# An FFN behind a grouped convolution: differences of x blocks and the low half of the odd blocks formed by GpSimd

## The reference

```python
def cond(x, c, weight, c_weight, bias):          # x (32, 64, 1024), 4 groups, 9 taps, padding 4
    out = lax.conv_general_dilated(x, weight, (1,), [(4, 4)], feature_group_count=4, ...)
    return out + einsum('nd,od->no', c, c_weight)[:, :, None] + bias[None, :, None]

def ffn(h, A_w, B_w, Wq_w, keys):                # last axis 1024; 64 experts of rank 8, top 16
    q = einsum('bsd,rd->bsr', h, Wq_w)
    scores = einsum('bsr,er->bse', q, keys)
    top_vals, top_idx = lax.top_k(scores, 16)
    gate = scatter of softmax(top_vals) to the 64 experts, 0 elsewhere
    z = einsum('bsd,nd->bsn', h, A_w)            # 64 experts x 8
    return 2.0 * einsum('bsn,on->bso', z * gate (per expert), B_w)

x = x + ffn(cond(x, ...), ...)
```

## Time and profile before

| | |
|---|---|
| median of 3 runs | 234.09 us (233.68 to 234.31) |
| span of the profiled execution, first to last instruction | 232.1 us |
| TensorE busy | 227.8 us, 98% |
| VectorE busy | 194.5 us, 84% |
| ScalarE busy | 99.5 us, 43% |
| GpSimd busy | 1.5 us, 1% |

### The profile page before, as it was taken

One profiled execution on the slowest core, in us unless ns is written; L12 is line 12 of the kernel. 1 busy time (PEld: TensorE's weight loads), 2 busy tenths in 40 slices (PEclk: granted clock), 3 DMA queues, 4 the chain that ended last, 5 costly groups with the idle time before them and its releaser, 6 DMA issues.

```text
span 232.1 us, 4019 instructions
## 1 busy us (share of the span) xinstructions
PE 227.8 (98%) x1381; PEld 203.3 (88%) x1381; DVE 194.5 (84%) x471; ACT 99.5 (43%) x246; POOL 1.5 (1%) x10
## 2 busy tenths in 40 slices
PE   7999999999999999999999999999999999999995
PEld 7898998898989889898998989889898989898884
DVE  2799899999999899998999899898998979847232
ACT  4997768246262352525334262532536242101000
POOL 2000000000000000000000000000000000000000
PEclk9999999999999999999999999999999999999999
DMA  6999064742744628173462825538281343554532
GB/s 199 372 406 395 25 194 127 274 133 93 211 151 104 218 82 270 60 211 144 95 235 74 252 82 148 187 88 263 67 272 69 60 169 90 186 145 130 180 135 92
DMA packets 23781, 38.79 MB, mean 167 GB/s; under 512 B 2768, under 2 KB 11856, under 8 KB 23760
## 3 DMA queue, kind: packets, MB, share of 16 engines
q1 hardware_dynamic: 23616, 38.45, 51.5%
q10 hardware_dynamic: 144, 0.08, 0.2%
HBM read 25.94 MB, written 12.58 MB: 166 GB/s over the span
## 4 chain that ended last, share of the span: by engine, by line
PE 90%; ACT 6%; DMA 2%; issue 1%; SPq 0%; DVE 0%; ACTq 0%
PE p_z L646 35%; PE p_out L684 13%; PE p_out L685 13%; PE p_out L692 13%; PE p_conv L600 10%; ACT h_c L395 3%; PE p_out L646 3%; PE p_conv L543 3%; DMA x_blk<-in_x_blocks 2%; ACT x_hi L359 1%; ACT a_hi L359 1%; PE p_z L668 1%; ACT h_hi L359 0%; PE p_z L692 0%; PE p_z L684 0%
## 5 line engine op out<-in xcount | busy, mean ns | idle before, releaser
L684 PE MATMUL p_out<-b_hi,zt_hi 128*128 128x512 f32 (+1 forms) x128 | 50.1, 392 | 0.0
L685 PE MATMUL p_out<-b_hi,zt_lo 128*128 128x512 f32 (+1 forms) x128 | 50.1, 392 | 0.0
L692 PE MATMUL p_out<-b_lo,zt_hi 128*128 128x512 f32 (+1 forms) x128 | 34.4, 391 | 0.0
L646 PE MATMUL p_z<-a_hi,h_lo 128*128 128x264 f32 x240 | 34.2, 285 | 0.0
L646 PE MATMUL p_z<-a_hi,h_hi 128*128 128x264 f32 x240 | 34.1, 285 | 0.0
L646 PE MATMUL p_z<-a_lo,h_hi 128*128 128x264 f32 x240 | 33.9, 284 | 0.0
L646 PEld LDWEIGHTS p_z<-a_hi,h_hi 128*128 128x128 f32 x240 | 32.0, 188 | 1.6 <-issue 0.4
L646 PEld LDWEIGHTS p_z<-a_hi,h_lo 128*128 128x128 f32 x240 | 31.3, 188 | 0.0
L646 PEld LDWEIGHTS p_z<-a_lo,h_hi 128*128 128x128 f32 x240 | 31.0, 188 | 0.0
L685 PEld LDWEIGHTS p_out<-b_hi,zt_lo 128*128 128x128 f32 x128 | 24.0, 188 | 5.6
L684 PEld LDWEIGHTS p_out<-b_hi,zt_hi 128*128 128x128 f32 x128 | 24.0, 188 | 5.6
(11 more groups left out here) (105 smaller groups left out, 258.1 us busy)
## 6 DMA issues: line engine op xcount, KB each, us to landing
x_nat<-in_x_rows SPq DMA_DIRECT2D x16, 512.0 KB, 5.0
out_dram<-x_nat SPq DMA_DIRECT2D x31, 256.0 KB, 3.3
x_blk<-in_x_blocks SPq DMA_DIRECT2D x14, 516.0 KB, 4.0
z_dram<-a_raw SPq DMA_DIRECT2D x64, 64.0 KB, 1.8
a_raw<-z_dram SPq DMA_DIRECT2D x16, 256.0 KB, 3.7
a_raw<-in_a_wq SPq DMA_DIRECT2D x8, 264.0 KB, 6.1
x_nat<-in_b_w SPq DMA_DIRECT2D x4, 512.0 KB, 8.6
x_blk<-in_x_blocks SPq DMA_DIRECT2D x2, 258.0 KB, 3.6
```

Of the source, the lines that this page charges most:

```text
L646: mm = nc.tensor.matmul(z_bank(t, b)[:, 0:HB], h[:, t % 2, r, :], a[:, r, b * HB:(b + 1) * HB], start=k == 0 and r == 0, stop=k == 2 and r ...
L684: nc.tensor.matmul(dst, zt_hi[:, t % 2, c, :], b_hi[:, c, cols], start=c == 0, stop=False)
L685: nc.tensor.matmul(dst, zt_lo[:, t % 2, c, :], b_hi[:, c, cols], start=False, stop=False)
L692: mm = nc.tensor.matmul(dst, zt_hi[:, t % 2, c, :], b_lo[:, c, start:stop], start=False, stop=c == JC - 1)
```

## The change

`differ` moves from VectorE to GpSimd, for all eleven tiles from the sixth on. GpSimd also forms the low half of the odd blocks of these tiles (512 columns), under a semaphore of its own, `s_xlo_odd`; VectorE's instruction there covers only the two differences (1024 columns). `conv_sum` waits for the new semaphore, `conv_pair` for the old one. A load into a buffer whose last tile was such a tile also waits for it. GpSimd takes the tiles in order: two differences as soon as the blocks have come, then the low half once ScalarE's high half is there.

```diff
@@ SP
                     sp.wait_ge(*x_lo_done(t - XB))
+                if t >= XB + TW:
+                    sp.wait_ge(s_xlo_odd, t - XB - TW + 1)
@@ GpSimd
+            def differ(t, ab):
+                if ab == 0:
+                    pool.wait_ge(*x_come(t))
+                blocks = x_blk[:, t % XB]
+                nc.gpsimd.tensor_tensor(blocks[:, XS + ab * XO:XS + (ab + 1) * XO], blocks[:, ab * NN:ab * NN + XO],
+                                        blocks[:, XE:XS], ALU.subtract).then_inc(s_xd, 1)
+
+            def split_odd(t):
+                pool.wait_ge(s_xhi, x_split_count(t))
+                nc.gpsimd.tensor_tensor(x_lo[:, t % 2, 0:XO], x_blk[:, t % XB, XE:XS], x_hi[:, t % 2, 0:XO].bitcast(F32),
+                                        ALU.subtract).then_inc(s_xlo_odd, 1)
+
+            for t in range(TW, NT):
+                differ(t, 0)
+                differ(t, 1)
+                split_odd(t)
@@ TensorE, conv_products
-                    if x is x_lo:
+                    if x is x_lo and part == 0:
+                        pe.wait_ge(s_xlo_odd, t - TW + 1)
+                    if x is x_lo and part > 0:
                         pe.wait_ge(*x_lo_done(t))
@@ VectorE, split_x
-                low(x_part(x_lo[:, t % 2], t, half), x_raw(t, half), x_part(x_hi[:, t % 2], t, half), s_xlo)
+                if t < TW:
+                    low(x_part(x_lo[:, t % 2], t, half), x_raw(t, half), x_part(x_hi[:, t % 2], t, half), s_xlo)
+                else:
+                    low(x_lo[:, t % 2, XO:3 * XO], x_blk[:, t % XB, XS:XS + 2 * XO], x_hi[:, t % 2, XO:3 * XO], s_xlo)
@@ VectorE, its order
-            differ(5, 0)
-            differ(5, 1)
...
-                if i + 3 < NT:
-                    differ(i + 3, 0)
                 copy_scores(i)
                 top_first(i)
-                if i + 3 < NT:
-                    differ(i + 3, 1)
                 take_first(i)
```

More of the change, by code:

```diff
@@ L149, in adaln_ffn @@
         s_xlo = sem("s_xlo")
+        s_xlo_odd = sem("s_xlo_odd")
         s_xd = sem("s_xd")
@@ L778, in split_ws @@
                 low(ws_lo[:, g % 2], ws_raw[:, g], ws_hi[:, g % 2], s_wslo)
[L780 to L785, removed]
             def add_shared(t, ab):
```

## The result

| | before | after |
|---|---|---|
| median | 234.03 us (4 runs, 233.68 to 234.31) | 243.8 us (4 runs, 243.1 to 244.16) |
| span of the profiled execution | 232.1 us | 242.4 us |

What follows compares the result with a forecast made beforehand. The prediction took TensorE's queue to bound the kernel; 232.1 us of span plus 2.5 and 1.4 for meetings of GpSimd and VectorE gave 236.0, with 2.0 around the span 238.0 us, range 233.6 to 244.5.

Steps and rivals of the forecast that it cites:

- What bounds the kernel, and what VectorE's relief is worth: Whole kernel: it ends when TensorE's queue ends, so 20 us taken from VectorE gain 0.
- The smallest reserve: Between VectorE's end of `q_t` and TensorE's load of it for the scores: 0.57 us, taken for all steps concerned.
- GpSimd's instruction: Each two-input GpSimd instruction of 512 columns: 1.2 us, within bounds of 0.68 and 1.60.
- The shift of the block load: In each loop step, `neg_max` to `turn_z` and the block load behind it come 0.47 us earlier.
- The sign named for the shift: In the changed profile, `neg_max` starts 0.26 us behind the maxima.
- How many meetings, and which: Nine loop loads, tiles 7 to 15: five arrive just ahead of `h_lo`, four inside it.
- What a meeting costs: At `h_lo` and `q_t`: one whole GpSimd instruction where GpSimd comes first, less the reserve; 2.5 plus 1.4 us.
- the five steps: Loop steps whose blocks arrive just ahead of `h_lo`: 0.5 us lost in each, 2.5 us together.
- the four others: Loop steps whose blocks arrive inside `h_lo`: 0.7 us each or 0, charged by half, 1.4 us.
- The second rival: Both GpSimd differences go first, the second between `h_lo` and `q_t`; all four open steps pay: 245.8 us, chance 0.17.
- The part ahead of the loop: Sixth tile: GpSimd's low half of 1.2 us hidden by 2 us before the shared convolution, no loss.
- a slower GpSimd: Rival: GpSimd instructions take 1.6 us, 0.4 more in seven steps on average, 240.8 us, chance 0.10.

Runs made afterwards that it cites:

- e_from8: Changed kernel, but the sixth and seventh tile stay wholly with VectorE and GpSimd starts later tiles' differences only behind `q_t`: 234.25 us, ratio 1.0004.
- e_halves: Changed kernel with each GpSimd difference cut into two instructions of 256 columns: 234.78 us, ratio 1.0028.
- e_both: Changed kernel with GpSimd's differences placed: behind `q_t` from the eighth tile, at VectorE's old places for the sixth and seventh: 235.31 us, ratio 1.0047.

## Why the prediction was wrong

*What bounds the kernel, and what VectorE's relief is worth.* Right. e_from8 takes 10.8 us of busy time from VectorE, and the ratio is 1.0004.

*The smallest reserve.* Right in place, and in size for most steps: all nine waits of the loop are for `q_t`; a hold of 0.49 us is free in eight steps (e_halves), one of 1.04 costs 0.4. The forecast took one step's 0.57 us for all. In the kernel before it is 0.56 to 0.58 in seven of the ten steps from 64 to 188 us, but 0.24 in the first and 0.44 and 0.46 in two more.

*GpSimd's instruction.* Put at 1.2 us, between 0.68 and 1.60; it takes 1.29 to 1.30 alone. The hold it causes is 1.04. Where GpSimd comes second I charged 1.28 for the hold and 0.7 for the step; it is 1.04 and 0.4.

*The shift of the block load.* Forecast 0.47 us; in most steps the load is issued 7.68 us behind the load of `q_t` instead of 8.26, so 0.58. About 0.1 of this is that the scores start sooner behind a weight load that TensorE had waited for. The sign named for the shift came out: `neg_max` starts 0.26 us behind the maxima in eight of the nine steps.

*How many meetings, and which.* Nine, five ahead of `h_lo` and four inside it, as forecast.

*What a meeting costs: the step that failed.* The forecast let one GpSimd instruction go first in the five steps, and charged the four others by half. The runs show strict turns: whoever waits goes next. So the second difference got in between `h_lo` and `q_t` in all five steps (1.25 to 1.44 us instead of 0.5), and the four others all paid. 5 x 0.5 = 2.5 became 6.6; 1.4 became 4 x 0.4 = 1.6. Together 3.9 became 8.2. The second rival had this mechanism, with a chance of 0.17 and 245.8 us; with its turns at 1.04 instead of 1.28 it comes out 5 x 0.24 + 4 x 0.3 = 2.4 lower, at 243.4. That this is so near the measured 243.8 is partly luck: its loop would lose 9.3 us and lost 8.2, and it has nothing ahead of the loop, where 1.7 were lost. I had its rule half in hand: the sentence that nothing says who comes next where both wait was true of what I had read, and I then took the milder answer without a row for it.

*The part ahead of the loop.* Put at nothing, with the low half of the sixth tile hidden by 2 us. I had asked only whether GpSimd would be in time, not whom it would hold. VectorE at 26 us, and again around 50 us:

```profile
26.51 1.26 DVE L904 SCALAR_TENSOR_TENSOR e_top<-sc_b,e_all 128x64 f32<-128x64 f32 x1
...
50.06 1.77 DVE L784 TENSOR_TENSOR zt_lo<-a_raw,zt_hi 128x512 fp32r<-128x512 f32 x1
51.76 2.31 DVE L784 TENSOR_TENSOR h_lo<-h_t,h_hi 128x1024 fp32r<-128x1024 f32 x1
```

An instruction of 64 columns took 1.26 us, because GpSimd formed the first differences as soon as their blocks had come, 19 us before VectorE used to. This stage has little reserve, and lost 1.7 us in the profiled execution: TensorE was 0.7 later by 39 us, 0.3 more at the gated z at 45.9 us, and 0.6 more at the output sum at 54.8 us, for which it waited 0.41. With this part placed or left with VectorE (e_both, e_from8) `e_top` takes 0.23 us at this place.

The direction was right, and the measured 243.8 us lies in the range of 233.6 to 244.5, but only because the range was wide: the sums worked out with the forecast's own mechanism went no higher than 239.4, or 240.8 with a slower GpSimd. The move of 9.8 us is two and a half times the 3.9 forecast.

## What to carry to other kernels

Moving element-wise work from VectorE to GpSimd is not free just because GpSimd is idle and the work is in time: list VectorE's instructions with two SBUF inputs that may run at that moment, and charge each with most of a GpSimd instruction (here 1.0 us of 1.3), with turns alternating while both have work. Then look only at the ones with a small reserve: shorter GpSimd instructions, a later start, or another order on VectorE each took the loss of the loop away, to 0.1 us or less. And where TensorE waits for nothing, relief of another engine has nothing to give back.

## What the runs showed of the hardware

A GpSimd subtraction of 512 columns holds a VectorE instruction with two SBUF inputs for 1.0 us, one of 256 columns for 0.5, a copy of 1024 columns for 0.8; a fill of 1024 columns (0.96 us) not at all; and an `h_c` with one input in PSUM, or a transpose, is not held. The Trainium skill's "SBUF — State Buffer", section "Who interferes with whom", says this of instructions that read on GpSimd and have two SBUF inputs on VectorE, and the runs agree with it. What they add is the size, each hold being 0.25 to 0.3 us shorter than that GpSimd instruction takes where nothing holds it (1.29, 0.74 and 1.10 us), and the order: in the five steps where both engines had work queued, the one that was waiting went next each time.

A held instruction shows in the profile as a long one, not as a wait: the 1.38 us of `q_t` are on VectorE's busy account, which is why the page's 194.5 us did not fall.
